# Delta attention, one core: the order of norms, token products, values and rates in one round, and an early table load

## The reference

```
xn = layernorm(x) * ln_w + ln_b                      # of a layernorm of the stream
q, k, v = xn @ Wq.T, xn @ Wk.T, xn @ Wv.T
alpha, aR   = sigmoid(xn @ Wa.T + ba), sigmoid(xn @ WaR.T + baR)   # rates, per feature
beta, gamma = sigmoid(xn @ Wb.T + bb), sigmoid(xn @ Wg.T + bg)     # gates, per head
for each token:
    kn = k / max(norm(k), 1e-12)
    r  = clip(v - S^T kn, -1, 1)                     # uses S before its update
    S  = alpha * S;  S += beta  * kn (v - S^T kn)^T
    R  = aR * R;     R += gamma * kn (r - R^T kn)^T
    o  = S^T q + R^T q
out = concat(o) @ Wo.T + x
```

## Time and profile before

| what | value |
|---|---|
| median of 3 runs (lowest, highest) | 4256.25 us (4253.89, 4263.85) |
| the profiled execution: own time, span | 4274.97 us, 4273.2 us |
| PE busy | 3434.2 us, 80% of the span |
| DVE busy | 2725.9 us, 64% |
| ACT busy | 1433.6 us, 34% |
| POOL busy | 919.8 us, 22% |
| delta attention's rounds | about 1068 us to 3672 us for 31 of them |

### The profile page before, as it was taken

How to read it: one execution, slowest core, us unless ns; L and a number is a source line. 1 busy time by engine, 2 the same in 40 slices (tenths; PEclk the granted TensorE clock), 3 DMA queues, 4 the chain that set the end, 5 groups by cost and what they waited for, 6 DMA issues and landing times. The chain is left out here.

```text
span 4273.2 us, 139676 instructions
## 1 busy us (share of the span) xinstructions
PE 3434.2 (80%) x61716; PEld 2480.6 (58%) x61716; DVE 2725.9 (64%) x5921; ACT 1433.6 (34%) x3221; POOL 919.8 (22%) x1018
## 2 busy tenths in 40 slices
PE   7833999995788888888888888888888888746777
PEld 4623667663566556666666566656666665524545
DVE  6834222222776777677767776777777677747887
ACT  1101111111344444444443444444444444321111
POOL 2216111211212222322232223222321232100000
PEclk9955999997799999989998999999988989877988
DMA  2163122222000000000000000000000000010000
GB/s 63 43 244 104 30 34 34 33 34 85 8 6 10 7 7 6 10 7 6 7 10 7 7 6 10 7 7 6 11 7 7 6 11 6 4 28 22 22 20 14
DMA packets 84279, 106.24 MB, mean 25 GB/s; under 512 B 14121, under 2 KB 74153, under 8 KB 83617
## 3 DMA queue, kind: packets, MB, share of 16 engines
q1 hardware_dynamic: 53280, 53.29, 4.2%
q0 software_dynamic: 19824, 23.03, 3.7%
q10 hardware_dynamic: 10576, 20.97, 1.4%
HBM read 59.29 MB, written 40.05 MB: 23 GB/s over the span
## 5 line engine op out<-in xcount | busy, mean ns | idle before, releaser
L970 POOL TENSOR_TENSOR da_M<-da_M,da_decay 128x512 f32<-128x512 f32 x256 | 276.0, 1108 | 723.0 <-DVE da_prev_end L1085 406.0
L1275 ACT COPY da_Ub<-da_U 32x256 f32<-32x256 f32 x1024 | 412.1, 402 | 17.1
L1110 DVE TENSOR_TENSOR da_eGn<-da_eGn,da_z 128x30 f32<-128x30 f32 (+14 forms) x960 | 352.7, 367 | 32.9
L1109 DVE TENSOR_TENSOR da_z<-da_eGn 128x30 f32<-128x30 f32 (+14 forms) x960 | 348.8, 363 | 27.6
L1556 PE MATMUL da_C<-da_Ub,da_Km 128*64 128x256 f32 x2048 | 306.5, 419 | 12.7 <-DVE da_M L1133 5.2
L759 PE MATMUL moe_ps_up<-moe_up,moe_zsT 128*128 x568 | 269.4, 597 | 1.4 <-ACT moe_zsT L678 1.4
L1388 PE MATMUL da_unit<-da_wx,da_xnT 128*128 128x512 f32 x512 | 255.5, 624 | 16.2 <-ACT da_xnT L1221 14.8
L777 PE MATMUL moe_ps_dn<-moe_down,moe_hT 128*128 x1136 | 257.0, 379 | 0.9 <-DVE moe_hT L637 0.9
L1454 PE MATMUL da_unit<-da_cum,da_sp 128*128 128x132 f32 x1024 | 195.5, 358 | 76.5 <-DVE da_ssm L1064 71.3
L1395 PE MATMUL da_unit<-da_xnT,da_wx 128*128 128x128 f32 x2048 | 243.8, 278 | 9.4 <-ACT da_eGn L1260 9.0
L1395 PEld LDWEIGHTS da_unit<-da_xnT,da_wx 128*128 128x128 f32 x2048 | 235.1, 193 | 17.8 <-ACT da_eGn L1260 17.8
(11 more groups left out here) (289 smaller groups left out, 7254.9 us busy)
## 6 DMA issues: line engine op xcount, KB each, us to landing
moe_zs<-moe_slots SPq DMA_DIRECT2D x71, 129.0 KB, 2.1
moe_up<-in_upT ACTq DMA_DIRECT2D x8, 1024.0 KB, 13.8
moe_down<-in_downT ACTq DMA_DIRECT2D x8, 1024.0 KB, 12.8
la_x<-in_x SPq DMA_DIRECT2D x16, 256.0 KB, 3.6
stream<-la_y SPq DMA_DIRECT2D x32, 128.0 KB, 2.3
moe_x<-stream SPq DMA_DIRECT2D x8, 512.0 KB
da_x<-moe_acc SPq DMA_DIRECT2D x128, 32.0 KB, 2.0
stream<-da_xz SPq DMA_DIRECT2D x128, 32.0 KB, 1.6
```

Source lines behind the costliest of these rows:

```text
L970: ins = nc.gpsimd.tensor_tensor(st_, st_, decay[:, par, rec, 2 * g:2 * g + 2].rearrange("p a b -> p (a b)").unsqueeze(2).to_broadcast([P, ...
L1109: c.link(tt(t, Xm[:, s + 1:C, s:s + 1].to_broadcast([P, below, s]), Xm[:, s:s + 1, 0:s].to_broadcast([P, below, s]), ALU.mult))
L1110: c.link(tt(Xm[:, s + 1:C, 0:s], Xm[:, s + 1:C, 0:s], t, ALU.add))
L1275: ins = nc.scalar.copy(Ub[rows_of(b), :, :, b, :], U[rows_of(b), rec])
```

## The change

On VectorE `norms_of_keys` moves ahead of group 0's first update and `norm_second`; `gram_out` of group 2 moves ahead of `clipped` of group 1; `norm_last` moves from ahead of `clipped` of group 1 to behind `decays`. On TensorE and ScalarE `growth(n, 1, 2)` comes ahead of `growth(n, 1, 1)`. On TensorE `turn_x` takes the place of the first half of `values`, so that the rates follow, and both halves of `values` come behind the rates; on ScalarE the copies move accordingly. The second half of `values` now waits until ScalarE has copied out the first. ScalarE gets one more activation per round, an exponential of one column, behind `rate_log`. SyncE clears the semaphores of the first stage at the beginning of this one.

```diff
-        GROWN = ((0, 1, 2), (1, 2, 0))
+        GROWN = ((0, 1, 2), (2, 1, 0))
@@ SP, start of the stage
+            for sem in consts["stale"]:
+                sp_.sem_clear(sem)
             load_x(0)
@@ DVE, period
                 if state:
                     clipped(i, par, 0)
+                if prepare:
+                    norms_of_keys(n)
+                if state:
                     update(i, 0, 0)
                 if norm:
                     norm_second(i + 2)
                 if prepare:
-                    norms_of_keys(n)
                     gates(n)
...
                     products(n, pn, 1, 1)
-                if norm:
-                    norm_last(i + 2)
+                    gram_out(n, pn, 2)
                 if state:
                     clipped(i, par, 1)
-                if prepare:
-                    gram_out(n, pn, 2)
-                if state:
                     update(i, 1, 0)
...
                     decays(pn, 1)
+                if norm:
+                    norm_last(i + 2)
+                if prepare:
                     gram_out(n, pn, 0)
@@ ACT
+            def exponents_next(n):
+                need(act, warmed, n)
+                nc.scalar.activation(spare[:], mhalf[:], ACT.Exp).then_inc(warmed, 1)
...
+                    growth(n, 1, 2)
                     growth(n, 1, 1)
-                    growth(n, 1, 2)
...
                     outputs(i, 2)
-                if prepare:
-                    values(n, 0)
-                if state:
-                    turned_outputs(i, 2)
                 if norm:
                     copy_xT(i + 2, par)
                 if state:
+                    turned_outputs(i, 2)
                     solved(i, 3, 0)
...
                     rate_log(i + 2)
+                if norm:
+                    exponents_next(i + 1)
                 if prepare:
                     turned_keys(n, 1)
+                    values(n, 0)
+                if state:
+                    outputs(i, 3)
+                if prepare:
                     values(n, 1)
-                if state:
-                    outputs(i, 3)
-                if prepare:
                     turned_keys(n, 2)
@@ PE
             def turn_x(n):
                 need(pe, xn_ready, n + 1)
-                need(pe, v_ready, (n - 1) * 2 + 1)
+                need(pe, gram_done, once(n - 1, 3))
...
             def values(n, par, half):
                 if half == 0:
-                    need(pe, gram_done, once(n, 3))
-                    need(pe, wr_ready, (n - 1) * NG + 2)
-                else:
                     if exists(n + 1):
                         need(pe, a_ready, (n + 1) * 4 + 3)
                     else:
-                        need(pe, v_ready, n * 2 + 1)
+                        need(pe, gram_done, once(n, 3))
+                    need(pe, wr_ready, (n - 1) * NG + 2)
+                else:
+                    need(pe, v_ready, n * 2 + 1)
                     need(pe, wr_ready, (n - 1) * NG + 4)
...
+                    growth(n, 1, 2)
                     growth(n, 1, 1)
-                    growth(n, 1, 2)
...
                     state_predicted(i, par, 3)
-                if prepare:
-                    values(n, pn, 0)
+                if norm:
+                    turn_x(i + 2)
                 if state:
                     turned_outputs(i, 2)
                     solve(i, 3, 0)
                     state_outputs(i, par, 3)
                 if norm:
-                    turn_x(i + 2)
                     rates(i + 2, par, 0)
...
                     turned_keys(n, 1)
+                    values(n, pn, 0)
+                if state:
+                    inner_outputs(i, par, 3, 1)
+                if prepare:
+                    state_rows(n, pn, 0)
                     values(n, pn, 1)
-                if state:
-                    inner_outputs(i, par, 3, 1)
-                if prepare:
-                    state_rows(n, pn, 0)
                     turned_keys(n, 2)
                 if state:
                     state_update(i, 3, 1)
```

More of the change, by code:

```diff
@@ L854, in delta_attention @@
         bg = m.sb("bg", [P, 2 * H]); nsig = m.sb("nsig", [P, 2 * H]); ssm = m.sb("ssm", [P, H]); kinv = m.sb("kinv", [P, H]); k2 = m.sb("k2", [P, H])
-        norm = m.sb("norm", [P, 2, H]); cc = m.sb("cc", [P, C]); ncT = m.sb("ncT", [P, C])
+        norm = m.sb("norm", [P, 2, H]); spare = m.sb("spare", [P, 1]); cc = m.sb("cc", [P, C]); ncT = m.sb("ncT", [P, C])
         A = m.psum("A", 1024); Bp = m.psum("B", 1024); Cp = m.psum("C"); unit = m.psum("unit", 1536)
@@ L859, in delta_attention @@
                  "tt_ready chain pool_chain cleared w_psum w_ready u_psum u_ready ub_ready p_psum wr_ready ds_psum s_updated dr_psum r_updated "
-                 "o_psum o_ready scaled oT_psum oT_ready out_psum out_ready added").split()
+                 "o_psum o_ready scaled oT_psum oT_ready out_psum out_ready added warmed").split()
         (loaded, x_loaded, var_ready, rstd_ready, z_ready, xz_ready, xz_stored, xn_ready, xT_psum, xT_ready, a_psum, a_ready, sp_ready, k_psum, k_ready, q_psum, q_ready,
@@ L863, in delta_attention @@
          tt_ready, chain, pool_chain, cleared, w_psum, w_ready, u_psum, u_ready, ub_ready, p_psum, wr_ready, ds_psum, s_updated, dr_psum, r_updated,
-         o_psum, o_ready, scaled, oT_psum, oT_ready, out_psum, out_ready, added) = [m.sem(n) for n in names]
+         o_psum, o_ready, scaled, oT_psum, oT_ready, out_psum, out_ready, added, warmed) = [m.sem(n) for n in names]
         sq = eG[:, 1, 0:DI].rearrange("p (h t) -> p h t", t=P)
@@ L1348, in period @@
                     rate_log(i + 2)
+                if norm:
+                    exponents_next(i + 1)
                 if prepare:
                     turned_keys(n, 1)
-                    values(n, 1)
+                    values(n, 0)
                 if state:
@@ L1354, in period @@
                 if prepare:
+                    values(n, 1)
                     turned_keys(n, 2)
@@ L1690, in period @@
                     turned_keys(n, 1)
-                    values(n, pn, 1)
+                    values(n, pn, 0)
                 if state:
@@ L1695, in period @@
                     state_rows(n, pn, 0)
+                    values(n, pn, 1)
                     turned_keys(n, 2)
```

## The result

The changed kernel takes 4304.99 us (median of 4 runs, 4297.15 to 4314.91), the kernel before 4260.05 us on the same occasions (4253.89 to 4268.74): a ratio of 1.0108, with a 95% interval of 1.0087 to 1.0130. The forecast was 4302.

The account below looks back on a forecast made before the run. No engine is full; the round is a loop that changes engines. Per round -3.9 + 4.7 + 0.6 = +1.4 us; +42 over thirty, -4 for one round, +8.5 for clears: +46, giving 4302 us, range 4222 to 4358.

Parts of the forecast that it names:

- the tail: The round's second part, from A to the next round's start: 9.1 us before, forecast 4.7 us longer, clock apart.
- the clears: SyncE's 33 semaphore clears ahead of the stage's first load: forecast +8.5 us once, with nothing to hide them.
- two signs of being wrong: Prediction wrong if PE's new wait is under 3 us, or start to A is over 5 us shorter.
- A: Instant in each round when the third piece of the rates starts its bias addition on DVE.
- The copy of v: PE's second half of the values waits for ScalarE's copy of the first: new wait of 5 to 6 us a round.
- The clock behind it: PE at half rate behind the new wait, values' product up to 3.6 us: 0 to +1.3 us a round, taken +0.6.
- Start to A: The round's first part: forecast -3.9 us a round, with all the ends -2 to -6.
- beside POOL: DVE's substitution steps no longer run while POOL scales the values: -0.6 us a round (0 to 1).
- the mask ahead of the clipping: DVE masks group 2's products before group 1's clipping: gain 0 to 1.7 us a round, taken 1.0.
- "Issue": Word on PE's waits at the token products, 103.0 us; part of a removed wait could come back under it.
- The gain from the norms: Key norms read first, so group 0's outputs come earlier for L1513: 1.8 to 2.3 us a round, taken 2.0.
- the faster rival: The first part shortens by 6.6 to 7 us against +4.7, about -2 a round: 4200 us, chance 0.20.

Follow-up runs that it names:

- only_values: Kernel before with only the rates' turn_x and matmuls moved ahead and both halves of the values behind them, on PE and ScalarE: 4382.82 us, ratio 1.0311.
- values_back: Changed kernel with the values' product and copy back in their old places, everything else as changed: 4169.32 us, ratio 0.9772.
- copy_first: Changed kernel with ScalarE's copies of the keys and of v's first half moved ahead of the logarithms: 4104.85 us, ratio 0.9629.
- filled: Changed kernel with 8 extra unused matmuls a round ahead of PE's wait for ScalarE's copy of v: 4253.32 us, ratio 0.9976.
- values_back_no_table: values_back without the exponential of one column, so the table load waits for the first sums again: 4139.57 us, ratio 0.9748.
- only_products: Kernel before with only group 2's products masked ahead of group 1's clipping and norm_last moved behind the decays: 4209.25 us, ratio 0.9896.
- only_norms: Kernel before with only VectorE's read of the key norms moved ahead of group 0's update and norm_second: 4193.79 us, ratio 0.9855.
- outputs_first: Changed kernel with ScalarE's copies of the keys, v's first half and group 3's outputs all ahead of the logarithms: 4079.05 us, ratio 0.9600.
- early_values: values_back with ScalarE's copies of the keys, v's second half and group 3's outputs ahead of the logarithms: 4099.05 us, ratio 0.9649.
- outputs_first_no_load: outputs_first without the exponential of one column, so the table is loaded when the first sums are there: 4078.35 us, ratio 0.9605.
- load_last: outputs_first with the exponential of one column behind the copies of v's second half and of the keys: 4073.23 us, ratio 0.9586.
- no_clears: Changed kernel without the 33 semaphore clears at the start of the stage: 4304.5 us, ratio 1.0104.

## Why the prediction was right, and where its terms were off

The mechanism was the one forecast. The first part of the round got shorter, and the tail longer by more, because the values' second half waits for a copy that ScalarE makes only after the logarithms. only_values shows that this part alone loses 3.1%, values_back that the rest without it gains 2.3%, and copy_first that it is the wait and not the order on PE. The sum of 46 us met the medians' 45, but that it came out so close was luck: the first part shrank by 2.1 us a round more than forecast, the tail grew by 1.5 more, and the clears cost 2 us instead of 8.5. Of the prediction's two signs of being wrong one appeared: the stretch from a round's start to A is 6.0 us shorter, and it had named 5. By its own figures (the first part losing over 4.9 us) the kernel should then have become faster; it did not, because the tail grew by 6.8 us and not by 5.3.

- *The copy of v.* Forecast 9.7 us from A to its end; the trace has 9.73 in the mean. The wait was forecast at 5 to 6 us and is 174.7 / 31 = 5.6. Right.
- *The clock behind it.* Forecast +0.6 with an end of +1.3. From the end of the copy to the next round it is 15.77 - 9.73 = 6.0 us, where 4.1 was the sum at the faster level: +1.9. The product behind the wait is nearly all of that, 3.68 us in the mean against 1.88 before, and filled gets the 1.9 us back. The mis-sized step is "At half rate its 1.8 us become up to 3.6, while the sums of the round's start, which paid before, may then be at 2.4 GHz". The sums did run faster (2.07 us for the 16 matmuls of L1461, 2.97 in the mean before), but they don't decide. In values_back they take 3.68 us in the mean, and the first clipping still ends 21.8 us behind the round's start, against 21.7 in the changed kernel. So nothing came back.
- *Start to A.* Forecast -3.9, measured -6.0 in the traces: -1.2 to the first clipping (forecast 1.0 for the table load; values_back and values_back_no_table differ there by 1.0), -1.5 to group 0's outputs (2.0), -2.5 to group 1's second solve (1.0), +0.4 to the mask of group 0 and -0.4 back behind it (0.7 lost), -0.8 beside POOL (0.6). The mis-sized term is the mask ahead of the clipping: in only_products alone that stretch is 1.9 us shorter, and only_norms gives another 0.8 there. "Issue" did not take the wait back: it fell, 103.0 to 52.9 us, and only_products shows that it is this edit that halves it.
- *Slips in the working.* The gain from the norms was read against the start of L1513; against the end of the copy that it needs (2411.18) the same rows give 1.0 to 1.3 us. The worst ends of the terms, with `norm_last`'s own 2.8, add up to 0 and not to -2, and the faster rival's parts add up to 7.3 us, not to 6.6 or 7. None of this changes which way the forecast points.
- *The parts do not need each other.* Norms alone 0.9855, products alone 0.9896, values alone 1.0311: added to 1 they give 1.006; the changed kernel has 1.0108. The difference, some 20 us, is about as wide as the intervals together; it can hold the early load, the new order of the growth parts, which no run has alone, and what the parts do to each other. In the late tail the early load stands on the path that decides, and where it doesn't decide (outputs_first with and without) it is worth nothing measurable.
- *The clears.* Forecast +8.5 us, measured 1.7 in VectorE's wait. The step that failed is the price, not "nothing hides it": 33 clears take 2.3 us at L920, and 1.7 of them do reach VectorE. In the earlier trace rows the loop at L452 takes 8.5 us although the median clear there has 25 ns; seven of its 32 steps from one start to the next take 0.7 or 1.4 us, 7.1 us together. In four later traces (only_values, early_values, outputs_first_no_load, load_last) the same loop at L452 takes 1.9 us. What holds SyncE up in the other traces stays open; it isn't the clears' own price.
- *The balance.* The profiled pair has +0.8 us a round, the medians 45 / 31 = about +1.4. The changed order is well measured: 85.65 us a round in its trace and 85.67 in that of no_clears. The profiled execution of before is the odd one. It is 15 us above its median, and its granted clock of 0.893 over the whole execution is below that of every run of this kernel between 4239 and 4276 us whose clock is on record (0.894 to 0.902). That this is the whole difference was not shown. With the measured terms the prediction's sum would be 46 - 30 x 0.6 - 6.5 = about 21 us, which is what the profiled pair shows (22), and half of what the medians do (45).

The trace agrees with the reading that a table load costs 1.28 us and no more: behind the logarithms, which end at 2463.16, it starts at 2463.18 and the exponential follows at 2464.48. The drain of 1.38 us that the Trainium skill adds (ScalarE: Activation LUTs, What ACT_TABLE_LOAD costs) appears in no run here (in all 14 traces the load takes 1.28 us). The load behind L1234 shows that the table for both functions that the Trainium skill names (ScalarE: Activation LUTs, Table sets: the hidden batching unit) isn't in use in this build.

Two versions take 4% less than the kernel before and 5% less than the changed one: outputs_first (0.9600) and load_last (0.9586).

## What to carry to other kernels

When one matmul product must wait until another engine has emptied its PSUM bank, look at where the copy that empties it stands in that other engine's order. Here it stood behind two logarithms, two table loads and a small exponential, and moving those behind the copy was worth 200 us. Follow one instant around the loop of engines and add up both halves: a change that shortens one half by 6 us loses if it lengthens the other by 7. A table load, or any work moved "off" a wait, gains only if the engine that does it has slack at the new place. And take the price of an operation from the median of its rows, not from the length of the loop that it stands in: that loop may be waiting for something else.

## What the runs showed of the hardware

Eight matmuls a round (a product of two steps, done twice, each step in two passes) whose result nobody reads made the kernel 1.3% faster than the changed one, because they kept the granted clock up through a wait: 0.96 over the rounds where it was 0.93. The half rate behind a wait of 5.7 us cost 1.9 us a round. And 33 semaphore clears on SyncE took 2.3 us at the start of the stage, in steps of 0.06 us in the median, and put off VectorE's first normalisation by 1.7 us; the same 33 took from 1.9 to 9.7 us at the other place in this program.
